# An LSTM with residual on one core: weights become the stationary operand of every gate, and the gates stay by units

## The reference

```python
xW = jnp.einsum('ntd,dk->tnk', x, Wx) + b          # x (4, 512, 256), Wx (256, 1024)
def step(carry, xw_t):
    prev_h, prev_c = carry                         # (4, 256) each
    a = xw_t + prev_h @ Wh                         # Wh (256, 1024)
    i, f, o = sigmoid(a[:, 0:H]), sigmoid(a[:, H:2*H]), sigmoid(a[:, 2*H:3*H])
    g = jnp.tanh(a[:, 3*H:4*H])
    next_c = f * prev_c + i * g
    next_h = o * jnp.tanh(next_c)
out = x + hs                                       # h0 = cond, c0 = 0
```

## Time and profile before

| what | value |
|---|---|
| median of 3 runs | 1062.07 us (1061.85 to 1062.7) |
| the profiled execution | 1062.23 us |
| its span, first to last instruction | 1060.4 us |
| TensorE matmul, busy | 867.7 us, 82% |
| TensorE weight load, busy | 635.6 us, 60% |
| VectorE, busy | 784.5 us, 74% |
| ScalarE, busy | 548.2 us, 52% |
| first weight load of the loop of steps | 15.35 us |
| end of the last h | 1055.47 us |

### The profile page before, as it was taken

One profiled execution on the slowest core, in us unless ns is written; L12 is line 12 of the kernel. 1 busy time (PEld: TensorE's weight loads), 2 busy tenths in 40 slices (PEclk: granted clock), 3 DMA queues, 4 the chain that ended last, 5 costly groups with the idle time before them and its releaser, 6 DMA issues.

```text
span 1060.4 us, 90187 instructions
## 1 busy us (share of the span) xinstructions
PE 867.7 (82%) x37888; PEld 635.6 (60%) x37888; DVE 784.5 (74%) x4899; ACT 548.2 (52%) x3586; POOL 0.7 (0%) x6
## 2 busy tenths in 40 slices
PE   4888888888888888888888888888888888888886
PEld 3666656656666666556566666665665666666654
DVE  5777777777777777777777777777777777777776
ACT  2555555555555555555555555555555555555554
POOL 0000000000000000000000000000000000000000
PEclk9999999999999999999999999999999999999999
DMA  3000000000000000000000000000000000000000
GB/s 91 6 7 6 6 6 6 7 6 6 7 6 6 7 6 6 6 6 7 6 6 7 6 6 6 6 6 6 6 7 6 6 7 6 6 6 6 6 6 7
DMA packets 32110, 8.74 MB, mean 8 GB/s; under 512 B 31584, under 2 KB 31584, under 8 KB 32096
## 3 DMA queue, kind: packets, MB, share of 16 engines
q1 hardware_dynamic: 31488, 8.41, 3.6%
q10 hardware_dynamic: 608, 0.14, 0.1%
HBM read 6.43 MB, written 2.10 MB: 8 GB/s over the span
## 4 chain that ended last, share of the span: by engine, by line
DVE 52%; PE 23%; ACT 15%; issue 8%; SPq 1%; DVEq 1%; DMA 0%
DVE turned_bank L299 40%; PE gates L372 23%; ACT tanh_o L213 8%; DVE h_pad L317 8%; ACT turned_bank L216 6%; DVE scan_both L304 3%; DVEq L333 1%; SPq L140 1%; DVE h_rows L273 0%; DMA wh_raw<-in_L_cond_Wh_dram 0%; SPq L144 0%; PE x_acc L364 0%; PE gates L358 0%; DVEq L272 0%; DVE wh L226 0%
## 5 line engine op out<-in xcount | busy, mean ns | idle before, releaser
L372 PE MATMUL gates<-wh,h_pad 128*32 128x64 f32 x32768 | 565.0, 221 | 175.7 <-DVE h_pad L317 174.2
L372 PEld LDWEIGHTS gates<-wh,h_pad 128*32 128x32 f32 x32768 | 482.6, 110 | 356.3 <-DVE h_pad L317 354.3
L299 DVE STREAM_TRANSPOSE turned_bank<-gates 128x64 f32<-128x64 f32 x2048 | 475.3, 263 | 163.3 <-PE gates L372 153.8
L204 ACT ACTIVATE tanh_f<-turned_bank 128x8 f32<-128x8 f32 x512 | 90.7, 177 | 431.1 <-DVE turned_bank L299 390.5
L364 PE MATMUL x_acc<-wh,zeros 128*32 128x256 f32 x1024 | 305.0, 379 | 0.3 <-issue 0.3
L349 PE MATMUL x_acc<-wx,x_units 128*32 128x128 f32 x2048 | 203.6, 284 | 9.4 <-DVE x_units L252 9.4
L211 ACT ACTIVATE scan_both<-turned_bank 128x8 f32<-128x8 f32 x1024 | 185.1, 181 | 48.5 <-DVE turned_bank L299 1.7
L317 DVE SCALAR_TENSOR_TENSOR h_pad<-tanh_o,turned_bank 128x4 f32<-128x4 f32 x1024 | 133.0, 158 | 73.3 <-ACT turned_bank L216 0.4
L310 DVE TENSOR_TENSOR_SCAN cell<-scan_both 128x12 f32<-128x12 f32 x1024 | 145.2, 182 | 0.0
L216 ACT ACTIVATE turned_bank<-cell 128x4 f32<-128x4 f32 x1024 | 143.7, 173 | 0.0
L349 PEld LDWEIGHTS x_acc<-wx,x_units 128*32 128x32 f32 x2048 | 94.9, 109 | 51.8 <-issue 9.3
(11 more groups left out here) (28 smaller groups left out, 9.1 us busy)
## 6 DMA issues: line engine op xcount, KB each, us to landing
x_next<-in_x_dram SPq DMA_DIRECT2D x256, 8.0 KB
x_here<-in_x_dram SPq DMA_DIRECT2D x256, 8.0 KB
out_dram<-y_rows SPq DMA_DIRECT2D x256, 8.0 KB
wx_raw<-in_L_cond_Wx_dram SPq DMA_DIRECT2D x8, 128.0 KB, 3.4
wh_raw<-in_L_cond_Wh_dram SPq DMA_DIRECT2D x8, 128.0 KB, 2.8
bias_raw<-in_L_cond_b_dram ACTq DMA_DIRECT2D x4, 32.0 KB, 3.0
h_rows<-in_cond_dram ACTq DMA_DIRECT2D x4, 1.0 KB
```

Of the source, the lines that this page charges most:

```text
L299: nc.vector.transpose(turned[k], gates[k][:, 0:W]).then_inc(gates_turned[k], 1)
L372: last = nc.tensor.matmul(gates[k][q * R:(q + 1) * R, 0:W], h_stationary(b, t), wh[:, b, q, columns_of(k)], start=False, stop=b == M - 1, ...
```

## The change

TensorE's operands are swapped in the steps. The weights of 32 units are now stationary (`wh[:, b, at:at + R]`, 128 x 32) and the 4 columns of h stream past (`h_ring[:, b, ...]`, 4 columns), so that a call gives 32 units x 4 rows with units on partitions. The gates need no transposes: ScalarE reads them from the PSUM banks of TensorE. A call covers one gate, one half and one quarter, so there are 64 calls in a step and not 32.

The banks F, A and B take a set of 4 steps (`SET`), 4 columns for each step and gate. The O gate has a bank for each half (`o_units`), and its tanh is two activations. TensorE starts with F and A on half 0 of h, waits for half 1, and goes on with F, A, B and O.

The input part is now made for sets of 4 steps: in step 0 of a set the bias goes into `x_acc` by matmul with the identity (`bias_part`, 256 columns), in steps 1 and 2 the two halves of x times Wx follow (`x_product`, 256 columns), in step 3 VectorE transposes the 128 x 256 result once (`turn_x_part`) and TensorE puts it into the banks F, A and B (`inject`). The O banks get theirs in step 0 of the next set (`inject_o`). `keep_busy` is 160 columns in steps 0 to 2 and 96 in step 3. TensorE's loop has 127 passes of 4 steps. ScalarE has two kinds of new copies: h of each step into `h_units` for the way out, and x of a set into `x_cur`. The weights `wh` are scaled in place on VectorE; nothing is permuted.

```diff
+    SET = STEPS // 2
+    SETS = STEPS // SET
+    SC = SET * N
...
+    PARTS = (((F, 0), (F, 1)), ((I, 0), (G, 0)), ((I, 1), (G, 1)))
...
+        scan_both = sb("scan_both", [128, M, 2 * (K * N + 1)])
+        scan_pairs = scan_both[:].rearrange("p m (g c) -> p m g c", g=2)
+        scan_add = [scan_both[:, m, 0:K * N] for m in range(M)]
+        scan_mult = [scan_both[:, m, K * N:2 * K * N] for m in range(M)]
...
+        h_ring = sb("h_ring", [128, M, SET, N])
+        h_units = sb("h_units", [128, M, STEPS, N])
...
-        gates = [ps(f"gates{k}", [128, 512]) for k in BANKS]
+        gates = [ps(f"gates{k}", [128, 512]) for k in (BF, BA, BB)]
+        o_units = [ps(f"o_units{m}", [128, 512]) for m in range(M)]
         x_acc = ps("x_acc", [128, 512])
-        turned_bank = [ps(f"turned_bank{k}", [128, 512]) for k in range(3)]
-        turned = [turned_bank[k][:, 0:W] for k in (0, 1, 2)] + [turned_bank[0][:, W:2 * W]]
-        tanh_c = [turned_bank[AB[m]][:, W:W + N] for m in range(M)]
+        tanh_c = [ps(f"tanh_c_bank{m}", [128, 512])[:, 0:N] for m in range(M)]
...
+        def group(t, k):
+            at = t % SET * N
+            return gates[k][:, 0:2 * SC].rearrange("p (g c) -> p g c", g=2)[:, :, at:at + N]
...
+            def copy_x(s):
+                x_set = x_units[:].rearrange("p (b c) -> p b c", b=M)[:, :, s * SC:(s + 1) * SC]
+                nc.scalar.activation(x_cur[:, :, 0:SC], x_set, ACT.Copy).then_inc(x_copied, 1)
+            def step(chunk, t, ahead):
+                now = chunk * STEPS + (t + 1)
+                act.wait_ge(gates_done[BF], now)
+                nc.scalar.activation(tanh_f[:], group(t, BF), ACT.Tanh).then_inc(tanh_f_done, 1)
+                for m in range(M):
+                    act.wait_ge(gates_done[AB[m]], now)
+                    ig = scan_pairs[:, m, 0:2, 1:1 + K * (N - 1) + 1:K]
+                    nc.scalar.activation(ig, group(t, AB[m]), ACT.Tanh).then_inc(tanh_ig_done[m], 1)
+                for m in range(M):
+                    act.wait_ge(o_done[m], now)
+                    nc.scalar.activation(tanh_o[:, m, :], o_units[m][:, t % SET * N:(t % SET + 1) * N], ACT.Tanh)
+                    act.wait_ge(cell_done[m], now)
+                    nc.scalar.activation(tanh_c[m], cell[:, m, :, K - 1], ACT.Tanh, scale=0.5).then_inc(tanh_done[m], 1)
+                nc.scalar.activation(half_d[:], cell[:, :, :, K - 1], ACT.Copy, scale=0.5).then_inc(kept_done, 1)
+                act.wait_ge(h_done[1], now + 1)
+                nc.scalar.activation(h_units[:, :, t, :], h_ring[:, :, t % SET, :], ACT.Copy).then_inc(h_copied, 1)
+                if ahead and t % SET == SET - 1:
+                    act.wait_ge(x_acc_done, chunk * SETS + (t // SET + 2))
+                    if t < SET:
+                        act.wait_ge(x_turned, chunk + 2)
+                    copy_x(t // SET)
+            act.wait_ge(x_turned, 1)
+            copy_x(0)
+            act.wait_ge(x_acc_done, 1)
+            copy_x(1)
+            with act.Fori(0, CHUNKS - 1) as k:
                 for t in range(STEPS):
...
+            def turn_x_part(s):
+                dve.wait_ge(x_acc_done, s + 1)
+                nc.vector.transpose(x_part_units[:], x_acc[:, 0:GC]).then_inc(x_part_turned, 1)
...
+                dve.wait_ge(h_copied, chunk * STEPS + STEPS)
+                nc.vector.transpose(h_rows[:], h_units[:].rearrange("p m t n -> p (m t n)")).then_inc(h_turned_back, 1)
...
                 if not first and t == 0:
                     turn_back(chunk - 1)
...
+                if not first and t == 2:
                     residual(chunk - 1)
...
+                if ahead and t == 1:
+                    dve.wait_ge(x_copied, chunk * SETS + 2)
                     dve.wait_ge(x_next_loaded, (chunk + 2) * (Q * DMA))
                     nc.vector.transpose(x_units[:], x_next[:]).then_inc(x_turned, 1)
...
-                turn(BF)
-                turn(BA)
-                turn(BB)
                 forget()
-                turn(BO)
                 update(0)
...
+            def bias_part():
+                for q in range(Q):
+                    nc.tensor.matmul(x_acc[q * R:(q + 1) * R, 0:GC], ident[:, q * R:(q + 1) * R],
+                                     bias_rows[:].rearrange("p g c -> p (g c)"), start=True, stop=False,
+                                     tile_position=(0, q * R), skip_group_check=True)
+            def x_product(b):
+                for q in range(Q):
+                    last = nc.tensor.matmul(x_acc[q * R:(q + 1) * R, 0:GC], x_cur[:, b, :],
+                                            wx[:, b, q, :, :].rearrange("p g c -> p (g c)"),
+                                            start=False, stop=b == M - 1, tile_position=(0, q * R), skip_group_check=True)
+                return last
+            def keep_busy(columns):
+                nc.tensor.matmul(x_acc[0:R, GC:GC + columns], zeros[:], bias_rows[:].rearrange("p g c -> p (g c)")[:, 0:columns],
+                                 start=False, stop=True, tile_position=(0, 0), skip_group_check=True)
+            def inject_o(m):
+                at = (O * M + m) * R
+                for q in range(Q):
+                    nc.tensor.matmul(o_units[m][q * R:(q + 1) * R, 0:SC], ident[:, q * R:(q + 1) * R],
+                                     x_part_units[:, at:at + SC], start=True, stop=False,
+                                     tile_position=(0, q * R), skip_group_check=True)
             def inject(k):
...
+                (gate0, m0), (gate1, m1) = PARTS[k]
+                gap = (gate1 - gate0) * M + (m1 - m0)
+                both = x_part_units[:].rearrange("p (g c) -> p g c", c=R)[:, gate0 * M + m0:gate0 * M + m0 + gap + 1:gap, 0:SC]
+                for q in range(Q):
+                    nc.tensor.matmul(gates[k][q * R:(q + 1) * R, 0:2 * SC].rearrange("p (g c) -> p g c", g=2),
+                                     ident[:, q * R:(q + 1) * R], both, start=True, stop=False,
                                      tile_position=(0, q * R), skip_group_check=True)
...
+            def step(s, t, ahead):
+                now = s * SET + (t + 1)
+                def add(b, bank_columns, gate, m):
                     for q in range(Q):
...
+                        at = gate * D + q * QD + m * R
+                        last = nc.tensor.matmul(bank_columns[q * R:(q + 1) * R, :], wh[:, b, at:at + R],
+                                                h_ring[:, b, (t - 1) % SET, :], start=False, stop=b == M - 1,
                                                 tile_position=(0, q * R), skip_group_check=True)
                     return last
+                def recur(b, k):
+                    for g, (gate, m) in enumerate(PARTS[k]):
+                        last = add(b, group(t, k)[:, g, :], gate, m)
+                    return last
                 pe.wait_ge(h_done[0], now)
                 recur(0, BF)
+                recur(0, BA)
                 pe.wait_ge(h_done[1], now)
                 recur(1, BF).then_inc(gates_done[BF], 1)
...
+                recur(1, BA).then_inc(gates_done[BA], 1)
+                recur(0, BB)
+                recur(1, BB).then_inc(gates_done[BB], 1)
+                if t == 0:
+                    for m in range(M):
+                        inject_o(m)
+                for m in range(M):
+                    for b in range(M):
+                        last = add(b, o_units[m][:, t * N:(t + 1) * N], O, m)
+                    last.then_inc(o_done[m], 1)
+                if ahead:
+                    if t == 0:
+                        pe.wait_ge(x_part_turned, s + 1)
+                    if t < SET - 1:
+                        keep_busy(160)
+                    if t == 0:
+                        bias_part()
+                    if t == 1:
+                        pe.wait_ge(x_copied, s + 2)
+                        x_product(0)
+                    if t == 2:
+                        x_product(1).then_inc(x_acc_done, 1)
+                    if t == SET - 1:
+                        pe.wait_ge(x_part_turned, s + 2)
+                        keep_busy(96)
+                        pe.wait_ge(tanh_ig_done[1], now)
+                        for k in (BF, BA, BB):
+                            inject(k)
+            pe.wait_ge(ident_made, 1)
+            pe.wait_ge(bias_made, 1)
+            bias_part()
             pe.wait_ge(wx_made, M)
...
+            pe.wait_ge(x_copied, 1)
+            x_product(0)
+            x_product(1).then_inc(x_acc_done, 1)
+            pe.wait_ge(x_part_turned, 1)
+            for k in (BF, BA, BB):
                 inject(k)
             pe.wait_ge(wh_made, M)
...
+            with pe.Fori(0, CHUNKS * SETS - 1) as k:
+                for t in range(SET):
                     step(k, t, True)
```

(22 more changed lines are left out.)

177 lines of the change are left out of this document (54 added, 123 removed).

## The result

The changed kernel takes 1312.95 us (median of 4 runs, 1298.13 to 1364.16; a fifth took 1283.74), the kernel before 1061.96 us (4 runs, 1060.5 to 1062.7). The ratio is 1.216, 95% interval 1.204 to 1.228; it is taken over the two fastest runs of the changed kernel, since its runs lie some 6% apart. Forecast were 906 us. The profiled execution is the slowest, 1364.16 us with a span of 1362.4 and a mean granted clock of 0.69; the other four had 0.80 to 0.84.

The account below looks back on a forecast made before the run. One dependent loop per step bounds the kernel, transposes and their bank waits being its largest piece. Start 15.35, 512 x 1.72 = 881, way out 4.9 plus 0.2, slow first steps 2: span 903.5, plus 1.8; forecast 906 us, range 878 to 1060.

Parts of the forecast that it names:

- The 7 ns pair: TensorE's gates: one weight load plus matmul of 4 columns costs 7 ns, 28 ns for four tiles; 14 the far end.
- 128 gate loads in 0.9 us: Sign in the new profile: TensorE's gate weight loads number 128 a step and take 0.9 us.
- rival 1: TensorE: a tile's next load starts only after its matmul, 34 ns a group of four pairs; about 958 us, chance 0.10.
- rival 2: TensorE's instruction supply: 14 ns a pair, 1310 us; the change turns to a loss at 10 ns; chance 0.09.
- Fits by 0.07: TensorE's gates, zero columns and input part take 1.63 us in steps 1 and 2, within a step of 1.70.
- F at 0.59: ScalarE's tanh of gate F starts 0.59 us after a step's first weight load; F's last matmul at 0.355.
- O ahead of the cell: Tanh of O, half 0, at 1.04 us (1.15 in step 0), before the cell's tanh at 1.27; otherwise the forecast fails.
- The full clock: TensorE was assumed to keep its full granted clock, 2.4 GHz, in all slices; forecast case with 7 to 8 ns pairs, 0.66.
- Rival 3: TensorE's clock falls to 1.2 GHz: step near 3.0 us, 1550 us; gain gone at 24% of the time; chance 0.15.
- the chain behind the gates: After tanh of F at 0.59 us: forget 0.80, scan 1.06, tanh of the cell 1.27, h 1.48, next load 1.70.
- the branch: End of TensorE's loop pass: 0.41 us from the last load before it to the next, making step 3 late by 0.04.
- 25 ns for each instruction of the whole array: Reading of the skill's ~60 cycle overhead: 25 ns a pair, 3.2 us a step, over 1600 us; ruled out, no chance.

## Why the prediction was wrong, point by point

- **The 7 ns pair, "128 gate loads in 0.9 us".** Wrong: 1.21 to 1.27 us in steps without a pause, 1.44 to 1.66 with one. The bursts of 8 were queued instructions; 28 pairs can be had like this, and then it is 8.35 ns. The prediction's argument against a slow supply was that right behind the loop's branch "nothing can have been queued for long"; but TensorE waited 0.31 us for h there, long enough. The price is the 34 ns a group of rival 1, which gave 958 us with it; its mechanism, a tile that takes so long, is excluded by the short loads and by the low clock. The mechanism is that of rival 2, supply, at 9.5 to 10 ns a pair without a pause and 10.8 in the mean of all steps, around the turning point of 10 that it gave.
- **"Fits by 0.07" and F at 0.59.** With the gates at 1.27 and not 0.90, TensorE's other work no longer fits into the step. F came at 0.65 in steps 0 and 4, and at 0.75 to 1.00 in the others, where a tile was held by the input part or a pause stood. The price of F itself was right: its 48 pairs reach their last start at 0.38 in steps 0 and 4, forecast 0.355.
- **O ahead of the cell ("at 1.04", 1.15 in step 0).** Wrong, 1.39 in step 0 and 1.61 in the timeline. The text named it as a mark of failure. It costs some 0.16 us in steps 0 and 4 and 0.03 in steps 1 and 2.
- **No term for pauses.** 0.12 us a step, about 60 us of a run, which no row of before shows: there the 64 loads of a step take 0.83 us from first to last start, whatever the step. A step at full clock is 2.06 and not 1.72 by these four points and a little of the loop's end; without the pauses the gain would not be gone (some 1.95 by the estimate above, against 2.03).
- **The full clock.** Wrong in two thirds of the profiled run. Rival 3 had it (the work in the array gone with the columns) and the price of a cold step, 3.0 against 3.01 measured. It got 0.15; its rows show full clock only beside the dense work that the change takes away, so it should have had more. Its bound of 24% of the time was passed by far.
- **Right:** the chain behind the gates, the branch (0.39 and 0.42 us from the last load ahead of it to the next in steps 3 and 7, forecast 0.41; but that last load comes at 2.06 and 1.96 and not 1.33, since the tanh of B that it waits for ends late), the transpose of 128 x 256 (450 ns against at most 0.47), the matmul of 4 columns (0.17 to 0.19 against 0.170), VectorE out of the chain. And 25 ns for each instruction of the whole array, which the overhead rule of the Trainium skill (TensorEngine Tiling (Array Packing), section Instruction Overhead) would give if read so, was rightly ruled out; but neither reading of it, per array or per tile, has the 8.35 ns that bound here.

The runs separate the two parts, as an estimate: with the clock held some 1093 us, 31 above before, and the rest up to the measured 1284 to 1364 is the clock. That the longer step itself lowered the clock is not shown: with loads of 16 columns the step is as long, and the clock was 0.993.

## What to carry to other kernels

Swapping operands so that few columns stream turns a matmul-bound step into an instruction-bound one: count instructions times 4.2 ns over the longest stretch without a wait, ask what the longer stretch pushes into the next step, and don't take a rate from a burst behind a wait. When columns go, ask what then holds the clock, and test it by adding zero columns on all tiles, since one cause can hide the other. Count a float32 call as two pairs, and keep a loop pass inside what stays loaded. Before calling a delay a property of a loop, list it over the longest period in the kernel: here the medians over 4 steps hid that the pauses keep to 8.

## What the runs showed of the hardware that was not expected

- TensorE's supply: 8.35 ns a pair of load and matmul in the long run, for loads of 32 and of 16 columns, for float32 and bf16, and at the low clock too where loads are short (103 ns). With float32 loads of 32 columns (157 ns at the low clock) it is 13.3 ns a pair there.
- Pauses of 0.16 to 0.37 us inside the gates of four steps in eight, mostly right behind one of SyncE's DMA issues, in the changed kernel and not in the kernel before.
- The granted clock is shown as full ahead of its first record, even where loads take 157 ns and not 108 (335.7 us in the kernel without zero pass). A duration of one shape tells the level there.
- With the same zero pass on four tiles, loads of 16 columns (0.993) and 100 pairs a step (0.990) had a higher clock than 128 pairs with 32 columns (0.922). Less work and more clock: why is open.
- A TensorE loop pass of some 2440 instructions is loaded anew (11.47 MB), one of some 1220 not.
